# New keys and their reciprocals asked for first on a semaphore of their own, and the first factors copied before the gathers

## What is computed

```python
q = _rope(_rmsnorm(einsum('bsd,ed->bse', x, Wq).reshape(bsz, 32, 32, 128), q_norm_w), pos)
k = _rope(_rmsnorm(einsum('bsd,ed->bse', x, Wk).reshape(bsz, 32, 8, 128), k_norm_w), pos)
v = einsum('bsd,ed->bse', x, Wv).reshape(bsz, 32, 8, 128)
kc = k_cache[block_table].reshape(bsz, 512, 8, 128)      # 16 pages of 32 keys for each sequence
vc = v_cache[block_table].reshape(bsz, 512, 8, 128)
k_all, v_all = concatenate([kc, k], axis=1), concatenate([vc, v], axis=1)
scores = einsum('bqhd,bkhd->bhqk', q, repeat(k_all, 4)) * SCALE   # 4 query heads share a key head
probs = softmax(where(valid, scores, -1e30))
o = einsum('bhqk,bkhd->bqhd', probs, repeat(v_all, 4))
return einsum('bse,de->bsd', o.reshape(bsz, 32, 4096), Wo)
```

## Time and profile before

| | us |
|---|---|
| median of 3 runs | 2443.51 (2442.0 to 2443.9) |
| the profiled execution | 2442.34 |
| its span, from the first to the last instruction | 2440.2 |
| TensorE matmuls busy in it | 2330.8 (96%) |
| VectorE busy | 1822.9 (75%) |
| ScalarE busy | 1229.0 (50%) |
| GpSimd busy | 512.5 (21%) |

### The profile page before, as it was taken

One profiled execution on the slowest core, in us unless ns is written; L12 is line 12 of the kernel. 1 busy time (PEld: TensorE's weight loads), 2 busy tenths in 40 slices (PEclk: granted clock), 3 DMA queues, 4 the chain that ended last, 5 costly groups with the idle time before them and its releaser, 6 DMA issues. The chain is left out here.

```text
span 2440.2 us, 50026 instructions
## 1 busy us (share of the span) xinstructions
PE 2330.8 (96%) x15564; PEld 2111.2 (87%) x15564; DVE 1822.9 (75%) x3082; ACT 1229.0 (50%) x2424; POOL 512.5 (21%) x537
## 2 busy tenths in 40 slices
PE   5999999999979999999999999999999999999999
PEld 4887777777859999999999999999999998888877
DVE  6659889889417877878787788787777787666654
ACT  3334444444316666666666666666666672111120
POOL 0002222222011222222222222222222214122100
PEclk8999999999989999999999999999999999999999
DMA  9845665566656888887878888888787888666522
GB/s 338 267 133 109 112 123 111 111 125 112 173 177 217 281 287 282 281 296 266 290 269 280 284 278 278 288 282 291 266 288 265 287 299 278 212 219 223 202 91 104
DMA packets 693166, 553.58 MB, mean 227 GB/s; under 512 B 369300, under 2 KB 608180, under 8 KB 688500
## 3 DMA queue, kind: packets, MB, share of 16 engines
q1 hardware_dynamic: 650628, 409.66, 54.3%
q0 software_dynamic: 36864, 134.23, 16.2%
q10 hardware_dynamic: 5616, 8.93, 1.1%
HBM read 449.17 MB, written 101.40 MB: 226 GB/s over the span
## 5 line engine op out<-in xcount | busy, mean ns | idle before, releaser
L1388 PE MATMUL ps<-at_pt,at_v_raw 128*128 128x128 f32 x4096 | 546.4, 277 | 0.0
L1467 DVE CUSTOM_DVE_ANT_0 at_sm<-ps,at_mask,at_factor 128x544 f32<-128x544 f32 x512 | 399.7, 781 | 149.6 <-PE ps L1354 105.7
L1388 PEld LDWEIGHTS ps<-at_pt,at_v_raw 128*128 128x128 f32 x4096 | 503.1, 194 | 0.0
L1540 ACT ACTIVATE at_pr<-at_sm,at_nm 128x544 f32<-128x544 f32 x512 | 384.4, 751 | 174.2 <-DVE at_nm L1467 162.1
L1527 ACT ACTIVATE at_pt<-ps 128x512 f32<-128x512 f32 x512 | 304.8, 595 | 261.8 <-PE ps L1363 190.1
L1354 PE MATMUL ps<-at_k_hi,at_q_hi 128*128 128x256 f32 (+1 forms) x1024 | 258.2, 333 | 74.2 <-DVE at_k_lo L1447 50.2
L1447 DVE TENSOR_TENSOR at_k_lo<-shared,at_k_hi 128x1088 fp32r<-128x1088 f32 x256 | 327.3, 1279 | 0.0
L1305 POOL DMA_INDIRECT at_v_raw<-v_cache,at_idx x256 | 290.7, 1136 | 113.5 <-issue 62.4
L1363 PE MATMUL ps<-constants,at_pr 128*128 128x128 f32 x2048 | 309.9, 274 | 0.0
L790 PE MATMUL ps<-xh,pr_hi 128*128 128x512 f32 x640 | 251.3, 393 | 0.0
L792 PE MATMUL ps<-xl,pr_hi 128*128 128x512 f32 x640 | 249.1, 389 | 0.0
(11 more groups left out here) (250 smaller groups left out, 3937.2 us busy)
## 6 DMA issues: line engine op xcount, KB each, us to landing
shared<-k_t SPq DMA_DIRECT2D x1024, 128.0 KB
qk_t<-pr_turned SPq DMA_DIRECT2D x320, 128.0 KB, 2.5
shared<-qk_t SPq DMA_DIRECT2D x64, 512.0 KB, 7.1
o_t<-at_ot SPq DMA_DIRECT2D x64, 512.0 KB
o_raw<-o_t SPq DMA_DIRECT2D x32, 1024.0 KB, 5.4
shared<-ri_d SPq DMA_DIRECT2D x32, 1024.0 KB, 7.9
f_w<-wqkv SPq DMA_DIRECT2D x12, 1024.0 KB, 5.6
s_k_in<-k_cache SPq DMA_DIRECT2D x16, 512.0 KB, 7.5
```

Of the source, the lines that this page charges most:

```text
L1388: e.matmul(sums(w, k), v_raw[:, q, c, g * D:(g + 1) * D], pt[:, jj % 4, c * P:(c + 1) * P], start=(k == 0 and c == 0), stop=False, skip_gr ...
L1467: e.tensor_tensor_reduce(out=sm[:, r, :], in0=scores(r), in1=mask[:, q, :], scale=factor[:, q, g:g + 1], scalar=3e38, op0=ALU.add, op1=ALU ...
L1540: e.activation(pr[:, w, k, :], sm[:, r, :], ACT.Exp, bias=nm[:, at], scale=-1.0, accum_out=su[:, at]).then_inc(s_e, 1)
```

## The change

It has two parts. In the first, a second pair of semaphores, `s_kn`, counts the reciprocals and the new keys, and `s_kp` counts the 16 pages alone. SyncE asks for the new keys right behind the reciprocals and ahead of the pages. On VectorE, the multiplication of the new keys waits for `s_kn`, in the projection for its one transfer and in the loop for two, and the high half of a batch's first two heads waits for `s_kp`. In the second part, GpSimd copies the first two batches' factors before it gathers. Lines behind the changed places have numbers lower by one after it.

```diff
--- before
+++ after
@@ project, SyncE @@
                     e.dma_start(kt[:, b, NPP, :],
-                                qk_t[b:b + 1, :, HK * P:HK * P + HK * S].rearrange("o d x -> (o d) x")).then_inc(s_kp[b], 16)
+                                qk_t[b:b + 1, :, HK * P:HK * P + HK * S].rearrange("o d x -> (o d) x")).then_inc(s_kn[b], 16)
@@ project, VectorE @@
                 new = kt[:, b, NPP, :]
-                e.wait_ge(s_kp[b], 16 * (NPP + 1))
+                e.wait_ge(s_kn[b], 16)
                 e.tensor_tensor(new, new, sums[:, b * HK * S:(b + 1) * HK * S], ALU.mult).then_inc(s_fixed, 1)
@@ attention, SyncE, load_keys @@
-                e.dma_start(inv[:, q, :], scales.rearrange("o g s -> o (g s)").broadcast_to([P, HK * S])).then_inc(s_kp[q], 16)
+                e.dma_start(inv[:, q, :], scales.rearrange("o g s -> o (g s)").broadcast_to([P, HK * S])).then_inc(s_kn[q], 16)
+                cols = slice(HK * P, HK * P + HK * S)
+                src = qk_t[bass.ds(b, 1), :, cols] if not isinstance(b, int) else qk_t[b:b + 1, :, cols]
+                e.dma_start(kt[:, q, NPP, :], src.rearrange("o d x -> (o d) x")).then_inc(s_kn[q], 16)
...
                         e.dma_start(kt[:, q, n + k, :], k_t[bass.ds(numbers[k] * P, P), :]).then_inc(s_kp[q], 16)
-                cols = slice(HK * P, HK * P + HK * S)
-                src = qk_t[bass.ds(b, 1), :, cols] if not isinstance(b, int) else qk_t[b:b + 1, :, cols]
-                e.dma_start(kt[:, q, NPP, :], src.rearrange("o d x -> (o d) x")).then_inc(s_kp[q], 16)
@@ attention, GpSimd @@
+            e.wait_ge(s_factors, 1)
+            for q in range(2):
+                e.tensor_copy(factor[:, q, :], factors[q][:, 0:HK]).then_inc(s_factor, 1)
             e.wait_ge(s_rot, NQU * NT // 2)
             e.wait_ge(s_rows, 1)
...
             e.memset(v_new[1][:, :, :], 0.0).then_inc(s_cleared_rs, 1)
-            e.wait_ge(s_factors, 1)
-            for q in range(2):
-                e.tensor_copy(factor[:, q, :], factors[q][:, 0:HK]).then_inc(s_factor, 1)
@@ attention, VectorE @@
+                    if g == 0:
+                        e.wait_ge(s_kp[q], (i + jj // PER + 1) * 16 * NPP)
                     if g == 0 and not (isinstance(u, int) and jj < PER):
                         e.wait_ge(s_fixed, i * 2 + jj // UB - 1)
-                    elif g == 0:
-                        e.wait_ge(s_kp[q], 16 * NPG)
...
-                    e.wait_ge(s_kp[q], (i + (j - 1) // PER) * 16 * (NPG + 1) + 16 * NPG)
+                    e.wait_ge(s_kn[q], (i + (j - 1) // PER) * 32 + 16)
                     e.tensor_tensor(new, new, inv[:, q, :], ALU.mult).then_inc(s_fixed, 1)
```

More of the change, by code:

```diff
@@ L805, in project @@
         sem = lambda n: sems.enter_context(nc.semaphore("pr_s_" + n))
-        kt, qk, s_kp, s_qk = keys
+        kt, qk, s_kp, s_kn, s_qk = keys
         s_ev, s_xlo, s_tab = first
@@ L1186, in attention @@
     QU = REP
-    NPG = NPP + 1
     W = 2 * P
@@ L1754, in build @@
         pair = lambda n: [ctx.enter_context(nc.semaphore(f"{n}{q}")) for q in range(2)]
-        keys = kt, qk, pair("s_kp"), pair("s_qk")
+        keys = kt, qk, pair("s_kp"), pair("s_kn"), pair("s_qk")
         place = nc.sbuf_base
```

## The result

The changed kernel takes 2338.62 us, the median of four runs (2337.66 to 2342.43 us), against 2443.16 us for the kernel before (four runs, 2442.0 to 2443.9). The ratio is 0.9575, with a 95% interval of 0.9559 to 0.9592: 104.5 us gained. The prediction said 2362 and 2346 to 2392.

The account below looks back on a forecast made before the run. TensorE, busy 96%, was taken as the bound, gaining only its waits and lost clock: loop 54.1 + 12.5 - 6 = 60.6, boundary 20.6, together 81.2 off 2442.34, plus 1.2 for the median: 2362 us; own range 2352 to 2372, 8-in-10 range 2346 to 2392.

Parts of the forecast that it names:

- T + 2.4: Attention loop: keys land on average 2.4 us after T, the end of the previous batch's own-value group.
- Rival (a): Loop: the page wait moves and keeps half, as transfers cannot follow shorter batches; loop gains 31, 2392 us; chance 0.20.
- (c): Loop part does nothing, the new wait being as long and passed on in full; only the boundary counts, 2423 us; chance 0.04.
- (d): Slower: the pages' landing slips by more than the 2.6 us the deadline gained, waiting at L1444; 2454 us; chance 0.03.
- The boundary: Projection to attention: second batch's rescaling and gathers start early, first score reduction at 713.1, not 733.67; 20.6 us gained.
- 16 us ahead of need: Boundary: own values are issued after SyncE's last page at 713, 16 us before they are needed.
- the first reduction's 9.41 us: Boundary: GpSimd copies the first factors last, so the first score reduction stands 9.41 us until 733.67.
- rival (b): Boundary: gathers collide with stores and TensorE waits in projection; loop 60.6, boundary 10, 2373 us; chance 0.09.
- the 17.6 us: Loop: part of the 84.2 us excess tied to no key wait, put to loop turns and short waits; not counted as gain.
- The clock's term of 12.5: Loop: about 1% of 1248 us of matmul work lost to half-clock spells after waits, counted as gained.
- 6 us for late batches: Loop: loss that remains, from about one late batch in ten and quarter-microsecond waits for L1447; subtracted from the gain.
- Rival (e): Loop: the unexplained 17.6 us goes too, since waits and slow clock may hide in records; 2344 us; chance 0.07.

Follow-up runs that it names:

- new_last: Changed kernel with SyncE asking for the new keys behind the pages again, both semaphores and waiting places kept: 2418.64 us.
- boundary_only: Changed kernel with the loop part undone: in the loop the rescaling of the new keys waits for all 16 pages too; 2418.64 us.
- after_again: The changed kernel once more, unaltered, beside two variants on the same chip: 2338.94 us.
- delay_3: Changed kernel plus three unused 128x512 multiplications on VectorE behind the rescaling in each of 62 batches, delaying the low half: 2402.74 us.
- loop_only: Changed kernel with the boundary part undone: rescaling for batches 0 and 1 waits for the pages too, GpSimd copies first factors last; 2384 us.
- factors_only: Changed kernel with both rescalings waiting for all pages as before; factors still copied first, new keys still asked for first: 2449.09 us.
- groups 3 and 4: Two of five groups of follow-up runs, each on its own chip; the kernel before had medians of 2443.1 and 2446.6 us there.
- one-engine shifts: Kernel with the loop change alone, plus eight long-met waits ahead of the loop on only TensorE, VectorE or ScalarE: 2385 to 2386 us.
- loop_only_shift: Kernel with the loop change alone, plus eight long-met waits ahead of the loop on each of TensorE, VectorE and ScalarE: 2360.17 us.
- rescale_late: Changed kernel with the first rescaling waiting for its batch's pages again; factors copied first, loop as changed: 2359.23 us.

## Why the prediction was right and wrong

**The bound and the mechanism: right.** TensorE gains what it waits and what its clock loses, and nothing else changed: the same instructions, the same busy time of VectorE. The keys land where they landed, T + 2.45 in the batch shown and T + 2.4 predicted; the wait at L1443 is half a microsecond as worked out; TensorE's wait for the low half is 1.6 us, under the 8 named; the mean clock is 1.00. Rival (a) fell, whose sign was a page wait over 1.5 us: 18.9 us in 36 waits, at a DMA share of 0.88. So did (c) and (d). new_last shows that the gain hangs on the order of requests, as the slack of the new keys said.

**The boundary: right**, 19.7 us against 20.6, and 21.0, 20.6 and 23.6 where runs isolate it (the last, boundary_only, has 20.1 of it at the first own-value group). The dates held within a microsecond. Two statements around it did not. The own values were said to be 16 us ahead of need; TensorE waits for them at the first values already, where its program puts that wait, and they were about 1 us late: 1.29 us of idle time in the profiled execution, 0.82 in after_again. And the change's GpSimd part, on which the prediction laid the first reduction's 9.41 us, is worth nothing: with the rescaling early, the factors would have come in time in the old order too.

**The collision of rival (b): half right.** While the gathers run beside projection, DMA share is 1.01 over 700 to 712, and the stores of own values land late. Over 690 to 725 the table of transfers of the changed kernel has

```profile
v_own<-pr_more SPq DMA_DIRECT2D x5, 256.0 KB, 5.8
v_own<-pr_stage SPq DMA_DIRECT2D x4, 256.0 KB, 4.4
```

where the kernel before has 2.0 us for both. The Trainium skill (DMA: Bandwidth & Descriptors, section Issuing engines are not separate DMA queues) has it that transfers issued by SyncE and GpSimd share the 16 engines and interleave; by that rule the stores were to be slowed, and the trace agrees. But TensorE is busy for all of the 12.00 us, and neither it nor ScalarE waits for a store behind 698: ScalarE empties a value tile every 2.72 us, as before. The four staging buffers are the likely reason; no run took one away. Keeping 20.6 was right.

**The loop: the failing term is the 17.6 us "that I tie to no key wait".** Most of it was the price of the very waits in the table. Reading the start of each step of scores in the kernel before, and not the idle column, its 84.3 us of excess are: 67.3 us in the 54 steps whose wait is recorded, 11.4 us in seven spells of half clock, 4.2 us in some sixteen steps that are 0.1 to 0.4 us long of their pace, and 1.4 us spread over the rest. Of the 67.3 the table of waits shows 54.0. The 13.3 us between them, 0.25 a wait, is the part that the idle column leaves out, and delay_3 measures it with a stall of known size: 0.88 us lost where 0.64 is recorded. It goes with the wait. So the sum should have read 67.3 + 11.4 and the short steps. The clock's term of 12.5 was sound.

Not all of the 54 are key waits. 41 of them (50.2 us recorded, 60.3 lost) stand at the step that reads the low half made behind the rescaling. The other 13 (3.8 recorded, 7.2 lost) stand half a batch away, at the step that is late in loop_only too, and 11 of them come 4.2 us behind a joint wait of ScalarE, like this one:

```profile
888.64 0.60 ACT L1527 ACTIVATE at_pt<-ps 128x512 f32<-128x512 f32 x1 [2.63 <-remote]
...
892.85 0.51 PE L1354 MATMUL ps<-at_k_hi,at_q_hi 128*128 128x256 f32 x2 [0.23 <-DVE at_k_lo L1447]
```

So some 7 us of the excess in that trace belong to the joint waits. The loop's gain doesn't rest on them: factors_only, which has none and whose keys are as late, has an excess of 89.0, with 69.6 us lost in 39 waits (60.1 recorded), all at the step behind the rescaling, and 16.2 us in eight spells of half clock.

The second, smaller error is what was left over: 6 us for late batches, against 4.0 in the profiled execution and 0.4 to 2.3 in the seven other kernels of groups 3 and 4, which have the same loop. So 84.2 less 4.0, 80.2 us, came where 60.6 stood. Of the 23.7 us between 2362.3 and 2338.6 the loop is 19.6, the boundary takes 0.9 back, and the last 5.0 is no mechanism: the prediction put the median 1.2 us above the profiled execution, and it is 3.8 below it.

Rival (e) named this, "waiting spells and slow clock may hide in records", and gave 2344 with a chance of 0.07; the time was its. That it still stood 5 us above the measured time is mostly the last 5.0 us just named. The clue was in the timeline, where the steps with a wait could have been set against undisturbed ones. The scores before those of 862.73, and two undisturbed ones in a row:

```profile
858.55 0.49 PE L1354 MATMUL ps<-at_k_hi,at_q_hi 128*128 128x256 f32 x2
...
880.97 0.49 PE L1354 MATMUL ps<-at_k_hi,at_q_hi 128*128 128x256 f32 x2
...
883.05 0.50 PE L1354 MATMUL ps<-at_k_hi,at_q_hi 128*128 128x256 f32 x2
```

A step takes 2.08 us undisturbed and 4.18 here: 2.10 us lost, with 1.85 recorded. By the same count VectorE's wait of 3.16 us was passed on less 1.06, and not less 1.3.

## What to carry to other kernels

When a stall of TensorE is to be priced, measure from one start to the next of the same instruction in the stalled and in an undisturbed step; the idle column leaves out a quarter of a microsecond of each stall here, and over 54 stalls that was 13 of the 84 us of excess. If an excess is left that no wait explains, count first what the recorded waits leave out, each by the same amount, before calling it a cost that stays. A wait for a set of transfers should stand at the first instruction that reads the set's last member, and a transfer that an earlier instruction needs should be asked for first, on its own semaphore; either without the other gives nothing (new_last, boundary_only). And two waits that lie side by side count once: half of the boundary's change was worth nothing by itself and nothing beside the other half.

## What the runs showed of the hardware

- The recorded idle time before a matmul is 0.24 to 0.25 us short of what the stall costs, for stalls that cost from 0.4 to 2.9 us (62 of 62 in delay_3; 13.3 us in 54 in the kernel before).
- Not every wait brings a spell of half clock behind it. The seven in the kernel before and the eight in factors_only each followed a stall that had cost 2.1 to 3.4 us, other stalls of that size brought none, and delay_3's 62 stalls of 0.88 us left the granted clock at 1.00.
- Beside gathers (changed kernel, DMA share 1.01 over 700 to 712), the landing of 256 KB stores took 4.4 and 5.8 us instead of 2.0.
- One loop can lose 0.45 us a batch more in one group of runs than in another, when VectorE and ScalarE wait 2 us together for TensorE at one place: loop_only and its one-engine shifts took 2384 to 2386 us on two chips, loop_only_shift 2360 on a third, rescale_late 2359 beside it. That the chip is the cause is likely and not shown. The kernel before takes 2438.7 to 2446.6 us on all five, and the two groups with joint waits have its lowest medians. Whether the changed kernel would lose it on such a chip, and be nearer to 2365, was not tried.
